# The end of a routed self-attention: the last unit's products with V issued once for four steps, in two halves of the keys

## What is computed

```python
s = sigmoid(x @ Ws)
vals, idx = top_k(s, 3)                      # all other heads weigh zero
scores = zeros_like(s).at[..., idx].set(vals)
attn = softmax((q * 64 ** -0.5) @ k.T)       # 4 batches, 8 heads of 64, 1024 tokens
out = attn @ v
proj = out @ Wo[h] + bo[h]                   # per head
x = x + tanh(g_ffn[1]) * sum_over_heads(proj * scores)
```

## Time and profile before

| | us |
|---|---|
| median of 3 runs | 2048.45 |
| lowest and highest | 2044.36, 2051.74 |
| the profiled execution | 2045.28 |
| its span in the trace | 2043.6 |
| PE busy | 1860.1 (91%) |
| start of the last unit's products | 2005.59 |
| start of the last `ot` on DVE | 2036.31 |

### The profile page before, as it was taken

The page is one execution under the profiler, slowest core; times in us unless marked ns, Lnnn a source line. Parts: engine busy times, 40 slices in busy tenths (PEclk is TensorE's granted clock), DMA queues, the critical chain, the costliest instruction groups (busy, mean ns, idle before and its releaser), DMA issues. The chain is left out here.

```text
span 2043.6 us, 61795 instructions
## 1 busy us (share of the span) xinstructions
PE 1860.1 (91%) x27105; PEld 1509.4 (74%) x27105; DVE 1202.8 (59%) x1703; ACT 1083.1 (53%) x1889; POOL 724.8 (35%) x982
## 2 busy tenths in 40 slices
PE   5899869999999999997799986899999999999986
PEld 3666558887887887876678865788778878888765
DVE  7787532432323333242455435888888888888783
ACT  4566433444434444342455533677677767777661
POOL 5777600000010000010333321456555565655441
PEclk9999979999999999998799997999999999999997
DMA  6222000000000000001201004322332142223110
GB/s 189 85 74 66 32 21 1 21 21 1 21 1 21 21 1 22 1 21 39 80 27 34 18 24 128 89 65 65 85 106 60 58 118 86 65 68 114 52 48 24
DMA packets 148839, 106.03 MB, mean 52 GB/s; under 512 B 22259, under 2 KB 144984, under 8 KB 148568
## 3 DMA queue, kind: packets, MB, share of 16 engines
q1 hardware_dynamic: 148568, 102.00, 16.7%
HBM read 76.33 MB, written 25.65 MB: 50 GB/s over the span
## 5 line engine op out<-in xcount | busy, mean ns | idle before, releaser
L2203 ACT ACTIVATE E_prob<-E_ps_s,E_negmax 128x1024 f32<-128x1024 f32 x256 | 284.7, 1115 | 143.2 <-DVE E_negmax L2517 142.8
L2517 DVE TENSOR_REDUCE E_negmax<-E_ps_s 128x1 f32<-128x1024 f32 x256 | 301.5, 1219 | 87.9 <-PE E_ps_s L2022 87.7
L2524 DVE STREAM_TRANSPOSE E_prob<-E_prob 128x1024 f32<-128x1024 f32 x256 | 304.0, 1226 | 23.7 <-ACT E_prob L2203 11.4
L2041 PEld LDWEIGHTS E_ps_o<-E_prob,E_vrep 32*64 32x64 f32 x15872 | 231.9, 130 | 69.1 <-ACT E_part L2229 56.3
L2041 PE MATMUL E_ps_o<-E_prob,E_vrep 32*64 32x128 f32 x15872 | 263.7, 274 | 16.6 <-issue 7.3
L1625 ACT ACTIVATE F_raw<-F_ps,ffn_scales 128x512 f32<-128x512 f32 x128 | 88.2, 689 | 288.2 <-PE F_ps L1535 288.2
L1535 PE MATMUL F_ps<-F_ha,ffn_w_rounded 128*128 128x512 f32 x1024 | 240.5, 395 | 0.0
L1535 PE MATMUL F_ps<-F_hb,ffn_w_rounded 128*128 128x512 f32 x1024 | 240.2, 395 | 0.0
L1535 PEld LDWEIGHTS F_ps<-F_hb,ffn_w_rounded 128*128 128x128 f32 x1024 | 192.3, 188 | 46.7
L1535 PEld LDWEIGHTS F_ps<-F_ha,ffn_w_rounded 128*128 128x128 f32 x1024 | 191.2, 188 | 48.0 <-issue 1.6
L2419 POOL TENSOR_TENSOR E_part<-E_part 128x512 f32<-128x512 f32 x93 | 119.3, 1283 | 253.4 <-ACT E_part L2229 253.4
(11 more groups left out here) (293 smaller groups left out, 3942.2 us busy)
## 6 DMA issues: line engine op xcount, KB each, us to landing
E_vrep<-E_v_all SPq DMA_DIRECT2D x128, 256.0 KB, 3.0
A_w_stage<-in_L_ffn_h_wT SPq DMA_DIRECT2D x16, 512.0 KB, 4.6
E_v_all<-E_vst SPq DMA_DIRECT2D x32, 256.0 KB, 2.2
F_x<-x SPq DMA_DIRECT2D x9, 512.0 KB, 3.7
A_x<-in_x SPq DMA_DIRECT2D x16, 256.0 KB, 4.2
x<-A_x SPq DMA_DIRECT2D x16, 256.0 KB, 2.2
x<-F_x SPq DMA_DIRECT2D x8, 512.0 KB, 2.9
C_x<-x SPq DMA_DIRECT2D x16, 256.0 KB, 5.5
```

The source lines that it names most:

```text
L2041: mm = pe.matmul(low[64 * j:64 * j + 64, g, :], vrep[rows, slot, KB // 4 * (quarter % 2) + k, dh * j:dh * (j + 1)], prob[rows, u % 2, :, j ...
L2203: act.activation(prob[:, s // UT % 2, s % UT, j, :], ps_s[:, j, :], ACT.Exp, bias=negmax[:, at:at + 1], scale=1.0, accum_out=den[:, 2 * c ...
L2517: dve.tensor_reduce(negmax[:, at:at + 1], ps_s[:, j, :], AX.X, ALU.max, negate=True).then_inc(d_max, 1)
L2524: dve.transpose(at, at).then_inc(d_t, 1)
```

## The change

`pv_whole` no longer takes a range of steps but a range of key blocks, and always covers the four steps (128 columns). It is called twice, for the blocks 0 to 15 and 16 to 31, as one accumulation (start at block 0, stop at block 31). Between the halves stand the transposes of the weights and the neighbour's projection. PE now waits for all of the unit's transposes before the first half; `part_in` at 4U is a value that PE had already waited for in the slot before. The counts of `e_slot` that ACT and DVE wait for move along. On DVE the neighbour's additions come ahead of `ot` of U.

```diff
-            def pv_whole(steps):
+            def pv_whole(blocks):
 
                 c = CP - 1
-                for k in range(KB):
+                for k in blocks:
                     for g in range(4):
                         rows = slice(32 * g, 32 * g + 32)
                         for j in range(2):
-                            mm = pe.matmul(low[64 * j:64 * j + 64, g, 32 * steps.start:32 * steps.stop],
+                            mm = pe.matmul(low[64 * j:64 * j + 64, g, :],
                                            vrep[rows, 2 * (c % 2) + 2 * k // KB, k % (KB // 2), dh * j:dh * (j + 1)],
-                                           prob[rows, 1, steps, j, 32 * k:32 * k + 32], start=k == 0, stop=k == KB - 1)
+                                           prob[rows, 1, :, j, 32 * k:32 * k + 32], start=k == 0, stop=k == KB - 1)
...
-            pe.wait_ge(d_t, 8 * U + 6)
-            pv_whole(slice(0, 3))
             pe.wait_ge(d_t, 8 * U + 8)
-            pv_whole(slice(3, 4)).then_inc(e_slot, 1)
+            pe.wait_ge(part_in, 4 * U)
+            pv_whole(range(KB // 2))
             pe.wait_ge(a_exp, 2 * STEPS * B)
             weights(U, lambda t: ps_s[:, 0, t * TOK:(t + 1) * TOK]).then_inc(e_slot, 1)
             pe.wait_ge(o_made, U)
             for pair in range(2):
                 out_proj(UNITS - 2, range(2 * pair, 2 * pair + 2), lambda t: ps_s[:, 1, t * D:(t + 1) * D]).then_inc(e_slot, 1)
+            pv_whole(range(KB // 2, KB)).then_inc(e_slot, 1)
             pe.wait_ge(o_made, U + 1)
...
-            act.wait_ge(e_slot, STEPS * B + 1)
+            act.wait_ge(e_slot, STEPS * B)
...
-                dve.wait_ge(e_slot, STEPS * B + 2 + 2 * half + pair)
+                dve.wait_ge(e_slot, STEPS * B + 1 + 3 * half + pair)
```

More of the change, by code:

```diff
@@ L2642, in _ @@
             U = UNITS * B - 1
[L2643 to L2649, removed]
             for h in range(2):
@@ L2654, in _ @@
                 add_y(0, pair, ps_s[:, 1, 512 * pair:512 * pair + 512].rearrange("p (t d) -> p t d", d=D))
+            dve.wait_ge(wrow_in, U + 1)
+            dve.wait_ge(e_slot, STEPS * B + 3)
+            dve.wait_ge(o_made, U)
+            by_group = "p (t g r) -> p g t r"
+            dve.tensor_tensor(ot[:, :].rearrange(by_group, t=UT, r=32), low.rearrange("p g (t r) -> p g t r", r=32),
+                              wrow[:, :].rearrange(by_group, t=UT, r=32), ALU.mult).then_inc(o_made, 1)
             for pair in range(2):
```

## The result

| | before | changed |
|---|---|---|
| median, us | 2048.7 (6 runs) | 2031.19 (6 runs) |
| lowest and highest | 2043.83, 2055.52 | 2022.87, 2032.24 |
| ratio, 95% interval | | 0.9907, 0.9888 to 0.9926 |
| the profiled execution, its span | 2045.28, 2043.6 | 2024.18, 2022.3 |
| products' start S | 2005.59 | 2000.07 |

The changed kernel is 17.5 us faster by the medians; 17.0 was forecast, 2031.4 against 2031.19. That they meet within 0.2 us is luck: the interval of the ratio alone leaves a gain of 15.2 to 22.9. The two traces differ by 21.3 us, and 5.5 of that lie ahead of S, where the change moves no work but PE's wait for the last transposes: they are the difference of two executions.

What follows compares the result with a forecast made beforehand. The end was taken as bound by loading of its code, with 1024 pairs becoming 512. Start, pace, blocks and pauses summed to `ot` at 2019.27 instead of 2036.31, 17.0 us earlier: 2048.45 - 17.0 = 2031.4, range 2025.5 to 2037.

Steps and rivals of the forecast that it cites:

- signs of being wrong: Pauses at other counts, their number not halved, clock 0.50 before 2017, or over 20 ns a pair in the second half.
- Start: First product of the last unit also waits for the last step's transposes: starts at 2005.89, 0.30 us late.
- Pace: Products of 128 columns take 16.4 ns a pair, so the first 236 pairs take 3.87 us, to 2009.76.
- Block C: Third code block (20 products, transposes, projection, 96 products): there at 2010.64, after a pause of 0.88 us.
- A: First code block of the last unit's sequence: the 108 products up to the first block boundary.
- D: Fourth code block, 128 products: loaded by 2014.38 at the latest, so no pause; runs 2.10 us, to 2017.54.
- C's work: Third code block's run: products 0.33, transposes 0.59, projection 1.95, return 0.36, 96 products 1.57; sum 4.80 us, to 2015.44.
- E: Last code block, 32 products and last projection: there at 2018.42, 2.98 after the crossing before it, pause 0.88 us.
- Behind it: After `ot` the chain is the same; two stores leaving early are worth 0 to 0.3 us, taken as 0.
- clock rival: PE's clock falls to 0.50 at the third code block: 3.5 us later, 2034.9; only later parts slow, 2032.6; chance 0.17.
- The second rival: Pauses belong to multiplications and their columns, not code loads: nothing saved, 2049.1, no change; chance 0.06.
- The slower rival: Second half's products run with fewer side by side; at 66 ns a pair 6.4 us slower, 2054.9; chance 0.03.

Runs made afterwards that it cites:

- count alone: Changed kernel with all 32 key blocks in one pass, weights' transposes and neighbour's projection behind it; ratio to before 0.9918, stretch 15.95 and 15.74 us.
- additions behind: Changed kernel with DVE's last `ot` ahead of the neighbour's two additions, as before the change; ratio to before 0.9923, stretch 13.57 us.

## Why the prediction was right, step by step

The mechanism is shown: load-bound before, and half of the instructions gives about half of the stretch. How near the total came is luck, since the traces alone spread the gain over 15.4 to 17.7. And one of the prediction's own signs of being wrong came true. It named the clock at 0.50 before 2017, and the clock was at 0.50 within a microsecond of S in all three traces of the changed kernel; it cost less than the rival had priced, for it came at another place (steps 3 and 7). By the steps, with the changed kernel's first trace:

1. **Start.** PE waited 2.41 ahead of S instead of 2.05, 0.36 longer (0.30 forecast), in all traces of the new waits.
2. **Pace.** 224 pairs in 3.42 are 15.3 ns a pair, where I had 16.4 (128 pairs with the last one's own length in it). At the high clock the first 236 took 3.58 (count alone). In the first trace they took 5.17, since the clock was low for the first 3.3 us of it, at 26.2 ns a pair.
3. **Block C** was forecast 4.75 behind S. With the high clock at S it was there 2005.72 - 2000.94 = 4.78 behind it, and 4.85, 4.85, 4.86 and 5.12 in the other such traces. In the first trace of the changed kernel it was 6.14, 1.4 more: with the low clock from S on, the 108 pairs of A take 2.8 instead of 1.6, and the load for C is asked for that much later. In its two others, where the clock fell after S, it was 5.1. The crossing into D then came 9.5 behind S, where the sum had 9.55, because C's work was shorter than the sum had it (step 4): two misses that cancel. The pause of 0.88 ahead of C was 0.97 in one trace and hardly there in two.
4. **C's work** was 4.80 by the sum and is 2010.58 - 2006.21 = 4.4 (2010.58 is 2009.11 and 96 x 15.3 ns). The return from the projection to the narrow products, which I had at 0.36, costs nothing that shows: the projection ends at 2007.29 + 1.89 = 2009.18 and the products start at 2009.11. The 0.36 of the earlier trace rows was idle time of the weight loads, over which PE still multiplied, so it did not belong in the sum; here the weight loads were idle for 0.33 in the same way. No pause ahead of D, as forecast.
5. **The mis-sized term.** E was forecast 2.98 behind the crossing into D with a pause of 0.88. It was there 2014.35 - 2010.58 = 3.8 behind it in the changed kernel's traces and 3.2 with the additions behind, and the pause was 1.8 and 1.3. The 2.98 had been read from the first boundary of before, with PE's position estimated at 13.1 ns a pair; the 3.47 to 3.74 between groups, which I had used for the bound, came nearer here. What the sum did not have are the early stores, which are under way when this load is asked for; whether they delay it is open (above, with DVE's order). It cost 0.8, and step 4 gave 0.4 of it back: 13.38 of stretch by the sum, 1.4 for block C, -0.4 for its work, 0.8 for E, make the 15.1 of the first trace; with 0.3 to 0.4 for block C instead of 1.4 they make the 14.10 of the two others.
6. **To `ot`**: 0.70 for the last 32 and 0.16 to DVE, 0.72 and 0.13 forecast.
7. **Behind it** nothing is gained but 0.1 to 0.3 for the stores; but where the clock falls around the last pause, 1.4 to 1.5 are lost in the last projection. This is the clock rival in part: it came true at the start in all three traces of the changed kernel and at the end in two. Its pace for the products, 24 ns, was nearly right, 26.2 measured, though by luck: it was scaled from the 18 ns of the group at 2017.20 in the earlier trace rows, read as one of 96 columns, while by the count (512 pairs in the first pass) that group holds 20 pairs of 96 and 108 of 32. The clock did not add up to the 3.5 us of the rival because the clock was back at 1.00 before C's projection.

The lower bound of the gain, 15.5, can't be had from the bounds of the steps, which give 15.9.

My attribution of the cover was wrong in one point. I had transposes and projection, 3.91 us, as taken off the path because they now lie over a load. The count alone has a stretch only 0.6 to 1.9 longer than the changed kernel's (0.6 of it DVE's order), since the next load is asked for when its predecessor is entered: work put into a block that is already as long as a load only moves all that follows. That the first load (D) covers the projection and the next (E) then comes later stood in my own step 5, so the sum was not hurt.

The second rival, with the rule of the Trainium skill ("Runtime: NRT & Kernel Launch", section "Instruction fetch mechanics") that the refill is mostly hidden, falls here: seven pauses with 10.5 and 12.2 us, 512 products with a quarter of the columns nearly as slow as whole ones. The page's block of 256 instructions is what the pauses' counts show; its room for 2048 instructions on TensorE would let many blocks of 128 pairs be waiting ahead, and in no trace here is more than the next block there. The slower rival, lost overlap behind the projection, needed 53 ns a pair; it was 15.3 there.

Left open: why S varies by 10 us from execution to execution, what decides that the same load takes 3.5 in one group and 4.0 in another, and whether the early stores delay the last one. No run here tells.

## What to carry to other kernels

Where an engine issues many short instructions with nothing else to wait for, count instructions as well as columns: pauses labelled "issue" at a fixed count mean that its code arrives slower than it runs, and then one wide call is worth as much as four narrow ones. Fewer calls help as long as such pauses are left (with 256 pairs none was); work moved between them helps only as far as it fills a pause. Compare such ends from a landmark inside the kernel: what lies ahead of it varied by 10 us here, more than any two variants with the same number of calls differ by.

## What the runs showed of the hardware

- A block of 128 pairs of weight load and multiply became usable 3.5 to 4.0 us after the one before had begun, where a pause marks both (2.8 to 4.0 by the pace of the pairs where PE ran into the block without a pause), and ran in 1.6 to 2.3 us: PE without other work was busy 40 to 67% of the time.
- The width of such a pair counts little: at the high clock 32 columns took 2.42 / 224 = 10.8 ns, 96 took 13.1 and 128 took 15.2 to 15.3; at the low clock 128 took 26.2.
- The granted clock fell to 0.50 for about 3.4 us or more within 2 us of S in eight of the fourteen traces, on both kernels; in the six others it was at 1.00 there. The wait of 2.0 to 2.4 us of PE ahead of S stands in all fourteen. Where the clock was low at the last projection (four traces), that took 1.4 to 1.8 us longer.
